# Linear attention and routed experts in one kernel: the inter-chunk products of a quad move into the next quad, and the state's sums with them

## Chip, cores and metric

One core of one Trainium2 chip runs the whole program. The metric is the device time of one execution in microseconds (us); lower is better. The kernel before was measured three times in a comparison: 363.81 us median, 362.58 to 365.19.

## What is computed

The input x is 8 sequences of 1024 tokens with 128 features, float32. It is normalized over the features (xn), and two branches are added to it:

```
x = L0_attn_x;  xn = _layernorm(x, axis=-1)
x = x + _L0_attn_ref(xn, W_qkv, W_o) + _L0_ffn_ref(xn, centroids, ln_g, ln_b, w1, b1, w2, b2)
# attention: 16 heads of 8 features, chunks of 64 tokens, keys normalized over their head
inter = einsum('bhde,bthe->bthd', S, q_c)
scores = where(causal, einsum('bthd,bshd->bhts', q_c, k_c), 0.0)
intra = einsum('bhts,bshd->bthd', scores, v_c)
S = S + einsum('bthd,bthe->bhde', v_c, k_c)          # the state, carried from chunk to chunk
# experts: each token goes to the one of 8 experts with the largest affinity
h = relu(layernorm(x)*g+b @ w1.T + b1);  out = sigmoid(affinity) * (h @ w2.T + b2) + x
```

## The kernel before

The tokens are 64 tiles of 128 tokens (two chunks of 64 each). Four tiles (four sequences, one pair of chunks) make a quad, and there are 16 quads, n = 0 to 15; even quads hold sequences 0 to 3, odd ones 4 to 7. Each quad is worked on in two halves, h = 2n and 2n+1, of two tiles each. All engines run one program each, written out by hand in the order in which it is issued, and they meet at semaphores; no scheduler moves anything. So what stands behind a waiting instruction on its engine waits too.

In the loop over h the engines do this for quad n:

- TensorE (PE): `scores(h)` for the half (64 small products into four PSUM banks `sc`); projections of the next quad: `kT_project(n+1)`, `q_project(n+1)`, `v_project(n+1)`, and `k_transpose(n+1)`; `state_step(n)`, what the two chunks of the quad add to the state; `inter_first(n)` and `inter_second(n)`, state times queries for the first and the second chunk; `products(h-1)`, masked scores times values of the half before; `output(n-1)`, the product with W_o; and transposes of rows (`x_transpose`) or, from quad 7, of the experts' weights (`w1_transpose`, `w2_transpose`). For odd n up to 7 come the expert affinities, and for n = 3, 5, 7, 9 three small products that rank the tokens.
- VectorE (DVE): `score_mask(h)` reads the score banks, multiplies by the causal mask and writes `pr`. PE can't begin `scores(h+1)` before it, because the banks are the same. For h below 18 ScalarE and GpSimd take one of the four banks (`score_copy`, `mask_scores`), and from quad 9 DVE takes all four. DVE also masks the state steps (`dstate_first`, `dstate_second`), makes the keys' variance `k_var(n+1)` from `sq`, its reciprocal root (`k_rstd`), the scaled values `vp` (`v_scale`), adds the output to x (`result(n-1)`), and does the layernorm's statistics, routing (`choose`, `count`, `ranks`, `places`, and from quad 9 the steps from `tiles_of_experts` to `slots_placed`) and, from quad 8, `b1_fold`.
- ScalarE (ACT): copies from PSUM to SBUF: `kT_copy`, `y_copy(n-1)`, `kn_copy(n+1)`, then `k_square` (writes `sq`), `k_root`, four `q_expand`, `q_copy`, half of the values' spreading (`values_across`), the transposed rows.
- GpSimd (POOL): up to quad 8 the state's two sums (`state_middle`, `state_end`), a bank of the mask, five tiles of layernorm and the values' other half; from quad 3 the scatter of rows to their expert's slots by indirect DMA (`send_rows`), paced by semaphores of other engines. From quad 9 the state's sums are DVE's.
- SyncE (SP): loads of tokens and expert weights, stores of results, each behind a semaphore.

PSUM has eight banks: four for scores, FA (queries, second state step, transposes), FB (keys, values, transposes) and two Y banks (first state step, then the attention of a quad, then its output). A bank is written anew only when the engine that reads it is done: `q_project` waits for `dstate_second`, `v_project` for `kn_copy`, the transposes into FA for `q_copy` and those into FB for `v_scale`.

After the last quad come 71 tiles of rows sorted by expert: load, transpose, up, relu, down, scatter-add. Their loop is not touched; only its entry (`se_scale`, `se_weights` of the first tiles) moves.

Of the kernel before, what the change touches and what calls it, by code (L numbers as in the profile page):

```python
# [19 lines left out]
def moe_attention_kernel(nc, x, w_qkv, w_o, centroids, ln_g, ln_b, w1, b1, w2, b2, out):  # L20
    B, L, D = x.shape
    E, F, _ = w1.shape
    P = 128
# [47 lines left out]
    with ctx:  # L71
# [25 lines left out]
        b2b = tokens[:, 0:E * D].rearrange("p (e d) -> p e d", d=D)  # L97
        lbb = tokens[:, CW:CW + E * D].rearrange("p (e d) -> p e d", d=D)
# [52 lines left out]
        dstate = sb("dstate", [P, NC, HALF, GW])  # L151
# [57 lines left out]
        banks = [ctx.enter_context(nc.psum_tensor(f"bank{i}", [P, BANK], F32)) for i in range(4)]  # L209
        FA, FB, Y = banks[0], banks[1], banks[2:4]  # L210
# [22 lines left out]
        def out_early(n):  # L233
            return n % 2 == 1 and n < 9
# [12 lines left out]
        def _(sp):  # L247
# [49 lines left out]
            for n in range(NQ - 1):  # L297
# [5 lines left out]
                if n == 6:  # L303
                    stored(n - 1)
                    sp.dma_start(lbb, ln_b.partition_broadcast(P)).then_inc(s("lb_in"), 16)
# [5 lines left out]
                if n and out_early(n):  # L311
                    store_quad(n - 1)
# [3 lines left out]
                if n and not out_early(n):  # L316
                    store_quad(n - 1)
# [28 lines left out]
        def _(pool):  # L346
# [79 lines left out]
            def state_middle(n):  # L426

                half = n % 2
                pool.wait_ge(s("dsta_sb"), n + 1)
                reach(pool, s("inter_ps"), n)  # L430
                if n < 2:
                    pool.tensor_copy(smid[:, :, :], dstate[:, 0, :, :]).then_inc(s("smid_ready"), 1)
                else:
                    pool.tensor_tensor(smid[:, :, :], state[:, half * HALF:(half + 1) * HALF, :], dstate[:, 0, :, :],
                                       ALU.add).then_inc(s("smid_ready"), 1)

            def state_end(n):
                half = n % 2
                pool.wait_ge(s("dstb_sb"), n + 1)
# [3 lines left out]
                pool.tensor_tensor(state[:, half * HALF:(half + 1) * HALF, :], smid[:, :, :], dstate[:, 1, :, :],  # L443
# [3 lines left out]
            for h in range(ROUTED):  # L447
                n = h // 2
                mask_scores(h)
                if h % 2 == 0:  # L450
                    state_middle(n)
                    state_end(n)
# [9 lines left out]
                else:  # L462
# [4 lines left out]
                    if n >= 3:  # L467
                        send_rows(2)
            for h in range(ROUTED, NH):
                n = h // 2  # L470

                pool.wait_ge(s("sc_ps"), h + 1)
                send_rows(1)
                if h % 2 == 0:
                    pool.wait_ge(s("av_ps"), h)
                    send_rows(1)
                    if n + 1 < NQ:
                        pool.wait_ge(s("q_ps"), n + 2)
                        send_rows(1)
                elif n + 1 < NQ:  # L480
                    pool.wait_ge(s("v_ps"), n + 2)
                    send_rows(1)
                    pool.wait_ge(s("out_ps"), n)
# [20 lines left out]
        def _(act):  # L504
# [129 lines left out]
            for h in range(NH):  # L634
# [3 lines left out]
                if h % 2 and more:  # L638

                    q_expand(n + 1, 0)  # L640
                    q_expand(n + 1, 1)
                if h and by_act(h):
                    score_copy(h)
                if h % 2 == 0:
                    if more:
                        kT_copy(n + 1)
                    if norm:
                        ln_root(n + 2)
# [5 lines left out]
                    if norm:  # L654
                        ln_norm(n + 2, (5, 6))
                    if n in (2, 4, 6, 8):
                        second_root(n // 2 - 1)
                else:
                    if more:
                        k_root(n + 1)  # L660
                        for j in range(2, J):
                            q_expand(n + 1, j)
                    if n < 8 and n % 2 == 1:
                        affT_copy(n // 2)
                    if more:
                        q_copy(n + 1)
# [65 lines left out]
        def _(dve):  # L732
# [129 lines left out]
            def dstate_first(n):  # L862
                dve.wait_ge(s("ds_ps"), n + 1)

                reach(dve, s("smid_ready"), n)
                nc.vector.tensor_tensor(dstate[:, 0, :, :], Y[n % 2][:, 0:HALF * GW].rearrange("p (i k) -> p i k", k=GW),
                                        bcast(smask[:, :], 1, HALF), ALU.mult).then_inc(s("dsta_sb"), 1)
# [611 lines left out]
```

## Time and profile before

| what | value |
|---|---|
| median of 3 runs | 363.81 us (362.58 to 365.19) |
| profiled execution | 363.22 us |
| its span | 361.4 us |
| what lies around the span | 1.8 us |
| granted TensorE clock | 0.992 of full over the span |
| quads 1 to 15 with the entry of the experts | 25.09 to 216.88 us of the span |
| experts' tiles | 216.88 us to the end |

The span is one execution by the hardware profiler; every duration below is of it. A quad is counted from the start of its `scores(2n)` on PE to that of the next.

### The profile page before, as it was taken

What the parts mean: (1) busy time and instruction counts of PE and PEld (TensorE: products, weight loads), DVE (VectorE), ACT (ScalarE), POOL (GpSimd) and SP (SyncE); (2) the same over time, 40 slices, a digit from 0 to 9 for tenths busy, and PEclk for the clock granted to TensorE, in tenths of its full rate; (3) what the DMA queues carried; (4) which work ended last, traced back from release to release, by engine and by line L of the source; (5) the groups of instructions that cost most, each with busy time, mean ns of one, the idle gap of its engine ahead of it and who ended that gap; (6) DMA issues with size and microseconds to landing.
All of it is one profiled execution on the core that took longest, in us unless ns stands there. A gap on an engine that the chain in (4) does not pass through costs nothing. (4 is left out here: it accounts for less than half of the span.)

```text
span 361.4 us, 17478 instructions
## 1 busy us (share of the span) xinstructions
PE 341.2 (94%) x6868; PEld 293.5 (81%) x6868; DVE 283.6 (78%) x799; ACT 241.7 (67%) x657; POOL 250.2 (69%) x245
## 2 busy tenths in 40 slices
PE   7799999989899999999999989999999999999990
PEld 7466776777587787777877878999999999999990
DVE  8887898898785988977878786788887778877760
ACT  4788677777667657666665735766677667766660
POOL 3388567889886865455455503888887888888884
PEclk9999999999999999999999999999999999999996
DMA  7403213021433233255233225555555555555420
GB/s 203 103 22 92 63 38 86 26 77 54 128 98 92 91 93 91 82 149 152 93 99 100 78 58 137 69 72 72 68 64 77 72 76 67 70 75 61 37 23 0
DMA packets 46705, 28.99 MB, mean 80 GB/s; under 512 B 5096, under 2 KB 44320, under 8 KB 46624
## 3 DMA queue, kind: packets, MB, share of 16 engines
q1 hardware_dynamic: 34352, 19.34, 19.6%
q0 software_dynamic: 12272, 8.54, 17.1%
q8 instruction: 55, 0.90, 1.1%
q14 instruction: 26, 0.21, 0.2%
HBM read 14.53 MB, written 13.78 MB: 78 GB/s over the span
## 5 line engine op out<-in xcount | busy, mean ns | idle before, releaser
L495 POOL DMA_INDIRECT out_dram<-qx,rows x71 | 112.7, 1588 | 36.0 <-issue 21.9
L695 ACT ACTIVATE qx<-sc,b1T 128x128 f32<-128x128 f32 x280 | 79.8, 368 | 40.4 <-PE sc L1424 40.4
L421 POOL DMA_INDIRECT slots_d<-rows,pos_i x64 | 62.8, 981 | 41.3 <-PE bank L1331 10.7
L857 DVE TENSOR_TENSOR pr<-sc,causal 128x1536 f32<-128x1536 f32 (+2 forms) x33 | 63.5, 1926 | 16.3 <-PE sc L1277 16.2
L1432 PE MATMUL bank<-tokens,qx 128*128 128x128 f32 x568 | 75.2, 276 | 0.7 <-ACT qx L695 0.7
L1424 PE MATMUL sc<-wide,tokens 128*128 128x128 f32 x560 | 74.1, 275 | 0.4 <-issue 0.4
L1432 PEld LDWEIGHTS bank<-tokens,qx 128*128 128x128 f32 x568 | 69.0, 192 | 1.1 <-ACT qx L695 1.1
L1424 PEld LDWEIGHTS sc<-wide,tokens 128*128 128x128 f32 x560 | 68.2, 192 | 0.6 <-issue 0.6
L1016 DVE COPY tokens<-xT 128x1024 f32 x71 | 53.3, 752 | 0.2 <-issue 0.2
L1277 PEld LDWEIGHTS sc<-qx,kT 32*64 32x64 f32 x2048 | 32.9, 130 | 16.8 <-issue 16.4
L1031 DVE SCALAR_TENSOR_TENSOR qx<-bank,rows,qx 128x128 f32<-128x128 f32 x71 | 24.8, 350 | 27.2 <-PE bank L1432 26.5
L1277 PE MATMUL sc<-qx,kT 32*64 32x128 f32 x2048 | 41.3, 279 | 2.3 <-issue 1.2
L538 ACT ACTIVATE qx<-bank,gmask 128x512 f32<-128x512 f32 x64 | 40.0, 679 | 0.9 <-PE bank L1203 0.8
L1331 PE MATMUL bank<-pr,vz 128*32 128x64 f32 x2048 | 37.4, 221 | 1.0 <-issue 0.8
L1331 PEld LDWEIGHTS bank<-pr,vz 128*32 128x32 f32 x2048 | 31.1, 110 | 6.0 <-issue 4.8
L413 POOL TENSOR_TENSOR pr<-pr,causal 128x512 f32<-128x512 f32 x18 | 22.9, 1273 | 7.6 <-ACT pr L569 7.2
L391 POOL TENSOR_SCALAR rows<-tokens,mv,rstd 128x128 f32<-128x128 f32 x35 | 27.5, 795 | 0.1
L1023 DVE SCALAR_TENSOR_TENSOR qx<-tokens,rows 128x128 f32<-128x128 f32 x71 | 24.5, 345 | 2.0 <-ACT rows L706 1.8
L603 ACT ACTIVATE y<-bank 128x512 f32<-128x512 f32 x16 | 9.6, 597 | 21.4 <-PE bank L1331 21.4
L1010 DVE TENSOR_SCALAR wide<-rows 128x128 f32<-128x128 f32 x71 | 19.6, 278 | 3.2 <-issue 2.7
L683 ACT ACTIVATE wide<-sc 128x128 f32<-128x128 f32 x69 | 20.2, 293 | 0.0
L1225 PEld LDWEIGHTS bank<-wqkv,xT 128*128 128x128 f32 x128 | 15.5, 191 | 4.4 <-issue 3.4
(167 smaller groups left out, 531.4 us busy)
## 6 DMA issues: line engine op xcount, KB each, us to landing
rows<-slots_d SPq DMA_DIRECT2D x71, 66.0 KB, 2.0
out_dram<-tokens SPq DMA_DIRECT2D x16, 256.0 KB, 2.7
tokens<-in_L_attn_x_dram SPq DMA_DIRECT2D x7, 512.0 KB, 4.2
w1raw<-in_L_ffn_w_dram SPq DMA_DIRECT2D x8, 256.0 KB, 3.3
w2raw<-in_L_ffn_w_dram SPq DMA_DIRECT2D x8, 256.0 KB, 2.9
out_dram<-qx,rows POOLq DMA_INDIRECT x71, 3.4
slots_d<-rows,pos_i POOLq DMA_INDIRECT x64
slots_d<-empty SPq DMA_DIRECT2D x9, 66.0 KB
```

The lines of the kernel that those rows point to most:

```text
L391: last = pool.tensor_scalar(rows[:, t, 0:D], xin[:, c, b, :], mv[:, t, 0:1], rstd[:, t:t + 1], ALU.subtract, ALU.mult)
L421: pool.indirect_dma_start(slots_d, bass.IndirectOffsetOnAxis(ap=pos_i[:, t:t + 1], axis=0), rows[:, t, :], None)\
L495: pool.indirect_dma_start(out_rows, bass.IndirectOffsetOnAxis(ap=xs[:, a, D + 2:D + 3].bitcast(U32), axis=0), ye[:, a, :], None, bounds_ch ...
L538: ins = nc.scalar.activation(qx[:, n % 2, :, j, :], FA[:, :].rearrange("p (i t) -> p i t", t=P), ACT.Copy, scale=gmask[:, j * DK:j * DK + 1])
L695: last = nc.scalar.activation(ht[:, k % 2, c * P:(c + 1) * P], inner(k)[:, c * P:(c + 1) * P], ACT.Relu, bias=b1T[:, bass.ds(e * FC + c, 1)])
L857: nc.vector.tensor_tensor(pr[:, h % 2, a:G, w].rearrange("p g (j t) -> p g j t", t=CH), sc[:, a * BANK:G * BANK].rearrange("p (g w) -> p g ...
L1016: nc.vector.tensor_copy(ws[:, k % 3, :], wts[:, bass.ds(e * WE, WE)]).then_inc(s("ws_ready"), 1)
L1031: nc.vector.scalar_tensor_tensor(out=ye[:, a, :], in0=banks[k % 2][:, 0:D], scalar=xs[:, a, D + 1:D + 2], in1=yb[:, k % 2, :], op0=ALU.mul ...
L1277: last = mm(SC[g][CH * up:CH * (up + 1), at:at + PAIRS * CH], kT[r, n % 2, tok], qx[r, n % 2, i, 2 * up:2 * up + 2, CH * c:CH * (c + 1)], ...
L1331: last = mm(Y[half][SW * g:SW * (g + 1), i * P + CH * c:i * P + CH * (c + 1)], vz[:, half, c, i, g, p, :], pr[:, h % 2, g, k:k + CH], star ...
L1424: last = mm(inner(k)[:, c * P:(c + 1) * P], ws[:, k % 3, c * P:(c + 1) * P], xsT[:, k % 2, :], start=True, stop=True)
L1432: last = mm(banks[k % 2][:, 0:D], ht[:, k % 2, c * P:(c + 1) * P], ws[:, k % 3, F + c * D:F + (c + 1) * D], start=(c == 0), stop=(c == FC ...
```

## The change

The order is rewritten on all engines.

- PE: `inter_first(n-1)` and `inter_second(n-1)` now stand in quad n, behind `kT_project(n+1)` and ahead of `state_step(n)`. Behind `products(2n-1)` come `k_transpose(n+1)`, `q_project(n+1)` and `v_project(n+1)` in a row, and then `scores(2n+1)`. `output(n-1)` always stands in the second half, first behind the scores. The products now clear a Y bank's accumulation, where `inter_first` did.
- Banks: Y, FA and FB lie in one tensor, so that the two state steps of a quad are neighbours and one DVE instruction of 128x512 masks both (`dstates`) in the place of two of 128x256. `dstate` has two buffers. In the last two quads, which need one step alone, it is still 128x256.
- State's sums: `state_end(n-1)` stands in quad n ahead of `state_middle(n)`, on POOL and on DVE.
- DVE: in the first half `score_mask(2n)`, the layernorm's inverse, `dstates(n)`, the sums, then `k_var(n+1)`, routing or slots, `b1_fold`, `k_rstd(n+1)`, `v_scale(n+1)`; in the second half `score_mask(2n+1)`, `result(n-1)` and the rest. In quads 1, 3, 5, 7 statistics and `result` stand ahead of `score_mask(2n+1)`.
- `b1_fold` waits for the weights' load and not for their transpose, and writes its product to `affT`.
- ACT: one `q_expand`, `k_root` and two more `q_expand` come in the first half, behind `k_square`; `score_copy(2n+1)`, the last `q_expand` and `q_copy` follow. `ln_root` comes first in a quad.
- POOL and SP: the scatters wait on other semaphores and end with quad 14; stores all stand behind `v_ps`; the first of the experts' broadcast loads comes two quads earlier.

The core of the diff:

```diff
-        dstate = sb("dstate", [P, NC, HALF, GW])
+        dstate = sb("dstate", [P, 2, NC, HALF, GW])
-        FA, FB, Y = banks[0], banks[1], banks[2:4]
+        Y, FA, FB = (banks[0], banks[2]), banks[1], banks[3]
...
 # POOL
                 if h % 2 == 0:
+                    if n:
+                        state_end(n - 1)
                     state_middle(n)
-                    state_end(n)
...
 # ACT, first half
                         kn_copy(n + 1)
                         k_square(n + 1)
+                        q_expand(n + 1, 0)
+                        k_root(n + 1)
+                        q_expand(n + 1, 1)
+                        q_expand(n + 1, 2)
...
 # DVE
+                    if more:
+                        k_var(n + 1)
...
-                    if n >= 8 and n + 1 < NQ:
+                    if n >= 8 and more:
                         b1_fold(n - 8)
-                else:
-                    if more:
-                        k_var(n + 1)
-                    score_mask(h)
                     if more:
                         k_rstd(n + 1)
                         v_scale(n + 1, FB)
+                    if n == NQ - 2:
+                        b1_fold(E - 1)
+                else:
...
+                    score_mask(h)
...
 # PE
                 if h % 2 == 0:
                     if more:
                         kT_project(n + 1)
+                    if n:
+                        inter_first(n - 1)
+                        inter_second(n - 1)
                     state_step(n)
                     if h:
                         products(h - 1)
-                    inter_first(n)
                     if more:
                         k_transpose(n + 1)
-                    if n and out_early(n):
-                        output(n - 1)
-                    if more:
                         q_project(n + 1)
+                        v_project(n + 1, FB)
                 else:
+                    if n:
+                        output(n - 1)
                     products(h - 1)
-                    if more:
-                        v_project(n + 1, FB)
-                    inter_second(n)
-                    if n and not out_early(n):
-                        output(n - 1)
```

TensorE in quad 10, from its first scores to the next quad's, before (`sc<-qx,kT` scores, `xT,wqkv` keys and then queries, `vp,kn` state step, `pr,vz` products, `qT,state` and `qT,smid` the inter-chunk sets, `ident,kT` the keys' transposes, `wqkv,xT` values, `wo,y` output):

```order
L1277 MATMUL sc<-qx,kT 64x128 x32
L1212 MATMUL bank<-xT,wqkv 128x512
L1258 MATMUL bank<-vp,kn 64x64 x16
L1331 MATMUL bank<-pr,vz 32x64 x32
L1298 MATMUL bank<-qT,state 64x64 x8
L1218 MATMUL bank<-ident,kT 128x128 x4
L1203 MATMUL bank<-xT,wqkv 128x512
L1277 MATMUL sc<-qx,kT 64x128 x32
L1331 MATMUL bank<-pr,vz 32x64 x32
L1225 MATMUL bank<-wqkv,xT 128x128 x4
L1309 MATMUL bank<-qT,smid 64x64 x8
L1340 MATMUL bank<-wo,y 128x128 x4
```

In both kernels the transposes of w1 and w2 follow, and then the next scores. The same stretch of the changed kernel:

```order
L1286 MATMUL sc<-qx,kT 64x128 x32
L1221 MATMUL bank<-xT,wqkv 128x512
L1306 MATMUL bank<-qT,state 64x64 x8
L1317 MATMUL bank<-qT,smid 64x64 x8
L1267 MATMUL bank<-vp,kn 64x64 x16
L1339 MATMUL bank<-pr,vz 32x64 x32
L1227 MATMUL bank<-ident,kT 128x128 x4
L1212 MATMUL bank<-xT,wqkv 128x512
L1234 MATMUL bank<-wqkv,xT 128x128 x4
L1286 MATMUL sc<-qx,kT 64x128 x32
L1348 MATMUL bank<-wo,y 128x128 x4
L1339 MATMUL bank<-pr,vz 32x64 x32
```

Both inter-chunk sets and the values' projection moved ahead of the second scores, and behind these stand four groups instead of six (w1 and w2 among them in both).

VectorE in quad 10, from the first mask to the last, before (`pr<-sc` the masks, `kvar<-sq` is `k_var`, `wide` the slots' step, `w1raw` or `affT` and `b1T` are `b1_fold`):

```order
L857 TENSOR_TENSOR pr<-sc,causal 128x2048
L866 TENSOR_TENSOR dstate<-bank,smask 128x256
L871 TENSOR_TENSOR dstate<-bank,smask 128x256
L879 TENSOR_TENSOR smid<-state,dstate 128x256
L884 TENSOR_TENSOR state<-smid,dstate 128x256
L989 TENSOR_SCALAR cnt<-cnt 128x8
L990 TENSOR_TENSOR wide<-cnt,iotk 128x568
L898 SCALAR_TENSOR_TENSOR w1raw,fold<-w1raw,tokens 128x128 x4
L902 TENSOR_TENSOR b1T<-smallT,fold 128x4
L829 TENSOR_REDUCE kvar<-sq 128x64
L857 TENSOR_TENSOR pr<-sc,causal 128x2048
```

And in the changed kernel:

```order
L864 TENSOR_TENSOR pr<-sc,causal 128x2048
L876 TENSOR_TENSOR dstate<-bank,smask 128x512
L885 TENSOR_TENSOR state<-smid,dstate 128x256
L892 TENSOR_TENSOR smid<-state,dstate 128x256
L836 TENSOR_REDUCE kvar<-sq 128x64
L998 TENSOR_SCALAR cnt<-cnt 128x8
L999 TENSOR_TENSOR wide<-cnt,iotk 128x568
L907 SCALAR_TENSOR_TENSOR affT,fold<-w1raw,tokens 128x128 x4
L911 TENSOR_TENSOR b1T<-smallT,fold 128x4
L841 RECIPROCAL krs<-kstd 128x64
L851 TENSOR_TENSOR vp<-bank,krs 128x512
L864 TENSOR_TENSOR pr<-sc,causal 128x2048
```

`kvar` moved ahead of the slots' step and of `b1_fold`, and `krs` and `vp`, which stood behind the second mask, now stand ahead of it.

## Rows read from the trace of the kernel before

**Rows 1.** Windows: length, busy us of PE, PEld, DVE, ACT, POOL; clock, DMA share, GB/s

```profile
104.02:117.20 13.18, 13.18 (x368) 9.96 (x368) 8.60 (x21) 9.14 (x18) 9.14 (x10) 1.00 0.39 108
25.09:129.57 104.48, 100.92 (x2858) 76.49 (x2858) 86.15 (x250) 76.97 (x156) 81.47 (x98) 1.00 0.26 74
129.57:205.35 75.78, 74.42 (x2101) 57.90 (x2100) 62.44 (x140) 49.36 (x97) 40.32 (x43) 1.00 0.35 105
205.35:216.88 11.53, 10.12 (x388) 8.89 (x388) 8.84 (x20) 4.77 (x9) 2.35 (x3) 1.00 0.31 80
```

**Rows 2.** Timeline of TensorE in quad 4 (start, duration, engine, line)

```profile
64.18 1.21 PE L1277 MATMUL sc<-qx,kT 32*64 32x128 f32 x64
65.31 1.13 PE L1212 MATMUL bank<-xT,wqkv 128*128 128x512 f32 x2
66.37 0.69 PE L1258 MATMUL bank<-vp,kn 64*64 64x64 f32 x32
66.99 1.10 PE L1331 MATMUL bank<-pr,vz 128*32 128x64 f32 x64
68.02 0.68 PE L1298 MATMUL bank<-qT,state 64*64 64x64 f32 x16
68.64 0.66 PE L1218 MATMUL bank<-ident,kT 128*128 128x128 f32 x4
69.13 1.02 PE L1203 MATMUL bank<-xT,wqkv 128*128 128x512 f32 x2
70.08 1.21 PE L1277 MATMUL sc<-qx,kT 32*64 32x128 f32 x64
...
72.25 1.16 PE L1225 MATMUL bank<-wqkv,xT 128*128 128x128 f32 x8
73.34 0.68 PE L1309 MATMUL bank<-qT,smid 64*64 64x64 f32 x16
...
75.11 1.09 PE L1169 MATMUL bank<-ident,rows 128*128 128x128 f32 x8
```

**Rows 3.** Timeline of VectorE in quad 10

```profile
144.25 2.29 DVE L857 TENSOR_TENSOR pr<-sc,causal 128x2048 f32<-128x2048 f32 x1 [1.41 <-PE sc L1277]
...
148.25 0.16 DVE L989 TENSOR_SCALAR cnt<-cnt 128x8 f32<-128x8 f32 x1
...
149.23 0.29 DVE L898 SCALAR_TENSOR_TENSOR w1raw<-w1raw,tokens 128x128 f32<-128x128 f32 x1
...
150.36 0.68 DVE L829 TENSOR_REDUCE kvar<-sq 128x64 f32<-128x512 f32 x1
150.95 2.28 DVE L857 TENSOR_TENSOR pr<-sc,causal 128x2048 f32<-128x2048 f32 x1
153.15 0.54 DVE L834 RECIPROCAL krs<-kstd 128x64 f32<-128x64 f32 x1
153.78 0.69 DVE L844 TENSOR_TENSOR vp<-bank,krs 128x512 f32<-128x512 f32 x1
```

**Rows 4.** Timeline of ScalarE in quad 10

```profile
148.38 0.60 ACT L598 ACTIVATE kn<-bank 128x512 f32<-128x512 f32 x1 [0.57 <-PE bank L1218]
149.01 0.63 ACT L551 ACTIVATE sq<-kn 128x512 f32<-128x512 f32 x1
```

**Rows 5.** Timeline of VectorE in quads 2 and 3

```profile
43.39 0.30 DVE L953 TENSOR_TENSOR tmp_nt<-rstd 128x16 f32<-128x16 f32 x1
...
46.09 1.75 DVE L857 TENSOR_TENSOR pr<-sc,causal 128x1536 f32<-128x1536 f32 x1
...
50.21 0.16 DVE L936 COPY scan<-ohb 128x8 bf16<-128x8 bf16 x1
...
52.93 1.73 DVE L857 TENSOR_TENSOR pr<-sc,causal 128x1536 f32<-128x1536 f32 x1
```

**Rows 6.** Timeline of TensorE, its inter-chunk set in quad 5 and products in quad 12

```profile
81.47 0.68 PE L1298 MATMUL bank<-qT,state 64*64 64x64 f32 x16 [1.14 <-DVE dstate L866]
...
171.76 0.76 PE L1331 MATMUL bank<-pr,vz 128*32 128x64 f32 x38 [0.45 <-issue]
```

More of the change, by code:

```diff
@@ L208, in moe_attention_kernel @@
         SC = [sc[:, g * BANK:(g + 1) * BANK] for g in range(G)]
-        banks = [ctx.enter_context(nc.psum_tensor(f"bank{i}", [P, BANK], F32)) for i in range(4)]
-        FA, FB, Y = banks[0], banks[1], banks[2:4]
+        bank = ctx.enter_context(nc.psum_tensor("bank", [P, 4 * BANK], F32))
+        banks = [bank[:, i * BANK:(i + 1) * BANK] for i in range(4)]
+        Y, FA, FB = (banks[0], banks[2]), banks[1], banks[3]
         RANK = HALF * GW
@@ L230, in inner, with with_affinities, with_ranks, step_of @@
             return SC[2 + k % 2] if k else FA
-        def out_early(n):
-            return n % 2 == 1 and n < 9
+        def with_affinities(n):
+            return n % 2 == 1 and n < 8
+        def with_ranks(n):
+            return n in (3, 5, 7, 9)
+        def step_of(n, c):
+            return dstate[:, n % 2, c ^ n % 2, :, :]
         block = ctx.enter_context(nc.Block())
@@ L637, in _ @@
                 norm = n + 1 < NCH
[L638 to L643, printed above, removed]
                 if h % 2 == 0:
+                    if norm:
+                        ln_root(n + 2)
+                    if h and by_act(h):
+                        score_copy(h)
                     if more:
@@ L658, in _ @@
                 else:
+                    if by_act(h):
+                        score_copy(h)
                     if more:
[L660 to L663, printed above, removed]
+                        q_expand(n + 1, 3)
+                        q_copy(n + 1)
+                    if with_affinities(n):
                         affT_copy(n // 2)
-                    if more:
-                        q_copy(n + 1)
                     if more:
@@ L1098, in _ @@
                         v_scale(n + 1, FB)
+                    if n == NQ - 2:
+                        b1_fold(E - 1)
+                else:
+                    if with_affinities(n):
+                        if stat:
+                            ln_stats(n + 3, range(4, B))
+                            ln_moments(n + 3)
+                        result(n - 1)
+                    score_mask(h)
+                    if n == NQ - 1:
+                        se_scale(0)
+                        se_scale(1)
+                    if n and not with_affinities(n):
+                        result(n - 1)
                     if n == NQ - 1:
@@ L1106, in _ @@
                         se_weights(1, e[3])
-                        se_scale(0)
-                        se_scale(1)
-                    if n and not out_early(n):
-                        result(n - 1)
                     if n == NQ - 2:
@@ L1118, in _ @@
                         second_rstd(n // 2 - 1)
[L1119 removed]
+                    if stat and not with_affinities(n):
                         ln_stats(n + 3, range(4, B))
                         ln_moments(n + 3)
[L1122 removed]
+                    if with_affinities(n):
                         aff_copy(n // 2)
```

125 lines of the change are left out of this document (57 added, 68 removed).

## The prediction

> **What bounds the kernel now.** I read the windows first, quad by quad, then TensorE's timeline, then VectorE's and ScalarE's around the waits of TensorE. The windows show PE busy for 100.92 of 104.48 us in quads 1 to 8 and for 74.42 of 75.78 in quads 9 to 14 [rows 1]: so PE's row of work fills the time, and the order of its instructions is what counts. The busy time alone proves little, for a matmul's end is modelled and covers short waits. So the timeline of PE in quad 4, where nothing waits for long, is to be read from start to start [rows 2]: scores 1.13, keys 1.06, state step 0.62, products 1.03, an inter-chunk set 0.61, keys' transposes 0.49, queries 0.95, values 1.09, the row transposes 1.03 with a short wait (the quad after starts at 76.14). The whole quad takes 11.96.
>
> What PE waits for, where it waits, is VectorE: 1.14 us for the masked state step in quad 5 [rows 6]. DVE is second: 86.15 of 104.48 us, and 62.44 of 75.78 [rows 1]. Per quad of 9 to 14 that is 10.4 of 12.6 us. So DVE has some 2 us to spare in a late quad, and less in the early ones. In the late quads it spends them waiting for scores (1.41 us ahead of a mask, [rows 3]). Nobody waits there, because two masks a quad, each 2.2 us, stand about half a quad apart. The experts' loop is not touched.
>
> **The change, part by part.** PE alone. The number of products stays. Set ahead, the two inter-chunk sets and the state step share one tile shape, and PE changes its shape less often. The price of a change of shape is in the difference of like groups (values 1.09 where a set of 64x64 follows, queries 0.95 where scores follow), about 0.1. I take 0.55 for a set that a set follows (ends: 0.50 and the 0.61 of the row), 1.0 for the values and 1.09 for the output, of the same form as the values. From the start of a quad: keys 1.13, first set 2.19, second 2.74, state step 3.29, products 3.91, keys' transposes 4.94, queries 5.43, values 6.38, second scores 7.4; then output 8.5, products 9.6, transposes 10.6, next scores at 11.7. So PE's own work would shrink from 11.96 to 11.7 us.
>
> The Trainium skill, "TensorEngine Tiling (Array Packing)", section "Key Properties", says that a change of tiling mode, other than of tile, drains TensorE. The trace agrees with that as far as the 0.1 us goes; by the rule alone the change would be a gain of some 0.2 us a quad. It does not say what the new order does to the other engines.
>
> The halves are no longer equal. Before, the second scores came about halfway (70.08 of 64.18 to 76.14, [rows 2]). Now the first half has 7.4 us and the second 4.3. DVE's mask of the second half must be done before the next quad's scores, since they write the same banks; it has 4.3 less the scores' 1.2, which is 3.1 us, for 2.28 us of mask, if DVE is free when the scores end.
>
> It is not free. In the first half it now runs `k_var`, which waits for `sq`, ahead of everything else that is left. Quad 10, from its start: the first mask starts at 1.35, when the scores end, and takes 2.21 to the next start [rows 3], to 3.6. The state step ends on PE at 3.29 + 0.69 = 4.0; `dstates` at 128x512 I price as `vp`, the same shape from PSUM, 0.69 [rows 3], to 4.75. The two sums, about 0.4 each, to 5.6. Now DVE waits: the keys' transposes end at 4.94 + 0.66 = 5.6, `kn` takes 0.60 and `sq` 0.63 with the small step between [rows 4], so `sq` ends at 6.9. This wait, 1.3 us, is new: before, the slots' step and `b1_fold` lay over it. Then `k_var` 0.59 from start to start, to 7.5; the slots' step 0.98 (148.25 to 149.23), to 8.5; `b1_fold` 1.13 (149.23 to 150.36), to 9.6; `krs` 0.63 and `vp` 0.63, to 10.9; the second mask 2.28, to 13.2; and PE starts at 13.3 where it was ready at 11.7 [rows 3]. What is queued behind that wait is the chain to the mask, and PE waits for it 1.6 us in each quad.
>
> Quads 9 to 14 by this walk: 13.3 in quads 10 and 11, 13.1 in 12, 13.4 in 13 (what stands in the slots' place there is 0.8 to 1.1); 13.4 in 14, where a second `b1_fold` (1.13) stands in it; 14.0 in 9, with ten small routing steps at about 0.17. The sum is 80.5 against 75.78: **4.7 us more**.
>
> Early quads. In 2, 4 and 6 the same chain has `choose` in it, 2.1 us (43.39 to 46.09 less the 0.59 of `k_var`), and a mask of 1.75 [rows 5]: 7.5 + 2.1 + 1.26 + 1.75 = 12.6, next scores at 12.8. In 3 and 5 DVE comes late from that: after the mask still `result` (0.6) and 2.72 us of counting, statistics and moments (50.21 to 52.93, [rows 5]). Its mask starts at 3.2 and ends at 4.95, `dstates` at 6.1, queries go at 6.2 instead of 5.6. `kn` comes behind two rows of layernorm and `y` on ACT, at 6.9, so values go at 7.6 and `sq` ends at 8.2. Then `k_var` 0.6, two small steps 0.5, `krs` and `vp` 1.26, statistics and moments 1.4, `result` 0.6, mask 1.75: 14.4, next scores at 14.5, in quad 5 14.7. Quad 7 has no layernorm left and PE sets its end, as in its window of 13.18 where PE is busy throughout [rows 1]: 13.1. Quad 1: 7.5 + 1.26 + 1.4 + 0.6 + 1.75 and the wait for the root, 13.3. Quad 8: `b1_fold` and a short mask, with the queries' copy on ACT at 11.3 and the transposes behind it, 12.3. The sum is 13.3 + 12.8 + 14.5 + 12.8 + 14.7 + 12.8 + 13.1 + 12.3 = 106.3 against 104.48: **1.8 us more**. The ends: with DVE a little faster everywhere, 102; with every wait of ACT behind DVE added once more, 110.
>
> The entry of the experts: in quad 15 `b1_fold` no longer stands ahead of the mask, about 0.9 us sooner for the second scores, but two inter-chunk sets now stand after them, about 0.6: 11.2 for 11.53 [rows 1], **0.3 less**.
>
> Pauses: PE stops now and then in the middle of a group for nothing that the profile names, 0.45 in quad 12 [rows 6]; such pauses add up to some 4 us in quads 1 to 14. My walks have none. Behind the second scores they lie beside DVE's lateness and cost nothing, in front of the keys' transposes they come on top. I add **0.8** (ends 0 and 2.5).
>
> Free of cost: one `dstates` for two masks saves 0.1 us of DVE (2 x 0.41 against 0.69) and lies in front of the wait for `sq`. The Trainium skill, "Perfetto Trace Analysis", section "Optimizing Scalar/DVE Operations", gives DVE some 125 ns of overhead an instruction on PSUM, which would be the same 0.1 us a quad; it would count only where DVE is the bound, and here the wait swallows it. The state's sums a quad later stay on POOL before quad 9, which has room; if they were late, the inter-chunk sets would wait. SP's stores behind `v_ps` and POOL's scatters on other semaphores lie beside PE; if the last rows landed later, the first expert tile would wait.
>
> The sum: 363.2 (the profiled execution, beside a median of 363.8) + 4.7 + 1.8 - 0.3 + 0.8 = 370.2 us.
>
> **The rivals.** *PE stays the bound (faster).* If `sq` comes early enough or DVE's steps shrink, the quads go at PE's own pace: seven even quads and 9, 11, 13 at 11.7, three with affinities at 13.0, quad 1 at 12.5: 168.5 against 180.3; less 11.8, with the pauses some 3 back: 354. For it speaks PE's full row; against it that the chain after `sq` adds up to 6.3 us at its shortest in quad 10, and 6.9 + 6.3 is over 11.7. It decides if that sum falls below 4.8.
>
> *The halves trade evenly (no change).* Late quads lose the 1.6 us, but early quads gain what PE waited for, and pauses vanish into DVE's lateness: quads 9 to 14 at 13.1 (78.6, 2.8 more), 1 to 8 at 12.7 (101.6, 2.9 less): 363. For it speaks that quad 5 alone waits 1.14 now [rows 6], and that most of the pauses now fall beside a wait.
>
> *ScalarE or GpSimd takes over (slower still).* `q_copy` comes behind seven instructions that wait on `sq` and `k_var`; POOL is busy 81.47 of 104.48 us [rows 1], and in quads 3 to 6 its scatters push its part of the mask back. If that adds 0.7 us in each of quads 1 to 8, the time is 376. It decides from the point where POOL's mask comes later than the products behind the next state step.
>
> **How the numbers follow.** A measurement of this kernel can tell about 1% from no change, 3.6 us. The forecast of 370 has a chance of 0.52 in itself, the still slower case 0.14, the even trade 0.19, and PE's pace, whole or in half, 0.15. Of the forecast's own range (366 to 374) almost all is slower by over 1%. The range that should hold 8 in 10 reaches down into the even trade and up to the third rival: 360.5 to 376. Faster by over 1% 0.15, within 1% 0.20, slower by over 1% 0.65.
>
> **What would show it.** Right, if in quads 10 to 14 PE waits 1 to 2 us ahead of each first scores, released by DVE's mask; if DVE's `kvar` waits about 1.3 us for `sq`; if these quads take 13.1 to 13.5 us, with PE idle where it was full; and if quads 3 and 5 have a wait of the queries for `dstate`. Wrong, if the late quads take below 12.3, or the second mask starts as soon as its scores end.

## The result, and the profile after

The changed kernel takes 375.95 us (median of 4 runs, 375.0 to 377.15) where the kernel before takes 363.33 on the same chip: a ratio of 1.0337, 95% interval 1.0302 to 1.0372, slower. The forecast was 370.2 with a range up to 376.0, so the direction holds and the size was 5.8 us short; the measured time lies 0.05 us inside the range. The profiled execution has a span of 373.3 us against 361.4. (Of the kernels below, kvar_late was profiled in its one slow execution, with a lower clock of TensorE for some microseconds; its time is that of the others, and its quads 0, 13 and 15 are not read.)

The windows of the changed kernel, cut where the first scores of quads 1, 9, 15 and 0 start, to be held against [rows 1] (the columns are the same):

```profile
core 0: us, PE busy (x) PEld busy (x) DVE busy (x) ACT busy (x) POOL busy (x), PEclk, DMA share, GB/s
25.59:134.01 108.42, 100.32 (x2842) 75.31 (x2841) 83.39 (x241) 76.88 (x156) 79.54 (x96) 1.00 0.25 71
134.01:215.94 81.93, 72.02 (x2101) 56.09 (x2101) 64.14 (x146) 50.81 (x100) 43.84 (x46) 1.00 0.33 99
215.94:229.01 13.07, 11.23 (x418) 9.69 (x419) 8.33 (x12) 3.10 (x6) 0.15 (x1) 1.00 0.35 90
12.95:25.59 12.64, 9.05 (x251) 6.50 (x250) 11.51 (x37) 10.81 (x23) 8.44 (x12) 1.00 0.15 44
```

Quads 1 to 8 take 108.42 us (104.48 before, +3.9), quads 9 to 14 81.93 (75.78, +6.15), quad 15 13.07 (11.53, +1.55), quad 0 12.64 (12.13, +0.5). The experts' loop takes what it took. PE, busy for 74.42 of 75.78 us before, now idles 9.9 of 81.93. Its timeline in quad 10 shows where:

```profile
148.71 1.20 PE L1286 MATMUL sc<-qx,kT 32*64 32x128 f32 x64 [1.63 <-DVE pr L864]
149.84 1.12 PE L1221 MATMUL bank<-xT,wqkv 128*128 128x512 f32 x2
150.89 0.68 PE L1306 MATMUL bank<-qT,state 64*64 64x64 f32 x16
...
152.47 0.62 PE L1267 MATMUL bank<-vp,kn 64*64 64x64 f32 x25 [0.32 <-issue]
153.02 1.10 PE L1339 MATMUL bank<-pr,vz 128*32 128x64 f32 x64
154.05 0.66 PE L1227 MATMUL bank<-ident,kT 128*128 128x128 f32 x4
154.54 1.02 PE L1212 MATMUL bank<-xT,wqkv 128*128 128x512 f32 x2
155.41 1.16 PE L1234 MATMUL bank<-wqkv,xT 128*128 128x128 f32 x8
156.49 1.43 PE L1286 MATMUL sc<-qx,kT 32*64 32x128 f32 x64
...
160.47 0.60 PE L1245 MATMUL bank<-ident,w2raw 128*128 128x128 f32 x4
162.38 0.87 PE L1286 MATMUL sc<-qx,kT 32*64 32x128 f32 x37 [1.31 <-DVE pr L864]
```

The first half runs from 148.71 to 156.49 and no matmul in it waits for another engine (the 0.32 is a pause in the middle of a group, see below); the second is done at 161.1 and then PE waits 1.31 us for the second mask, where [rows 2] had no long wait. DVE's timeline of the same quad, to be held against [rows 3]:

```profile
149.95 2.29 DVE L864 TENSOR_TENSOR pr<-sc,causal 128x2048 f32<-128x2048 f32 x1 [0.79 <-PE sc L1286]
153.13 0.69 DVE L876 TENSOR_TENSOR dstate<-bank,smask 128x512 f32<-128x512 f32 x1 [0.89 <-PE bank L1267]
153.73 0.41 DVE L885 TENSOR_TENSOR state<-smid,dstate 128x256 f32<-128x256 f32 x1
154.28 0.42 DVE L892 TENSOR_TENSOR smid<-state,dstate 128x256 f32<-128x256 f32 x1
156.05 0.69 DVE L836 TENSOR_REDUCE kvar<-sq 128x64 f32<-128x512 f32 x1 [1.34 <-ACT sq L559]
...
156.84 0.78 DVE L999 TENSOR_TENSOR wide<-cnt,iotk 128x568 f32<-128x568 f32 x1
...
158.71 0.54 DVE L841 RECIPROCAL krs<-kstd 128x64 f32<-128x64 f32 x1
159.34 0.69 DVE L851 TENSOR_TENSOR vp<-bank,krs 128x512 f32<-128x512 f32 x1
159.95 2.28 DVE L864 TENSOR_TENSOR pr<-sc,causal 128x2048 f32<-128x2048 f32 x1
```

From `kvar` on DVE has no gap, and its mask ends at 162.2, when PE may go. In [rows 3] the second mask ends at 153.23, 2 us ahead of the next scores (155.18); here it ends 0.15 us ahead of them. The waits over the attention part (engine, line, released by: us in total, times, longest):

```profile
DVE kvar L836 <- ACT sq L559: 20.8, 14, 3.3
...
PE sc L1286 <- DVE pr L864: 11.1, 9, 1.6
PEld bank L1234 <- ACT kn L606: 9.3, 14, 0.7
```

The first row is the wait that the change adds (before it was 1.5 us in all), the second is its price on PE. The price is paid late: quads 9 to 14 have 8.7 us of the first and 7.2 of the second, quads 1 to 8 have 12.1 and 2.5. The third row costs nothing: it is the load of the values' weights, beside the queries' matmuls. The chain that ended last has changed owners too; its shares are by engine, and DVE had 2% and PE 5% of it before:

```profile
issue 30%; PE 28%; DVE 20%; POOL 12%; ACT 8%; POOLq 1%; DVEq 0%; ACTq 0%
```

### The profile page after: what moved, and what is told of

Its sections match the earlier page's. It is cut to its first block, busy times and chain, and to the rows that moved or that the text cites. A ratio compares the mean times of both kernels' runs of the same rounds, so it can differ in the third digit from the quotient of the medians.

```text
span 373.3 us, 17460 instructions
## 1 busy us (share of the span) xinstructions
PE 338.4 (91%) x6868; PEld 290.6 (78%) x6868; DVE 282.8 (76%) x786; ACT 241.8 (65%) x657; POOL 249.6 (67%) x244
## 4 chain that ended last, share of the span: by engine, by line
issue 30%; PE 28%; DVE 20%; POOL 12%; ACT 8%; POOLq 1%; DVEq 0%; ACTq 0%
POOL out_dram L503 12%; DVE pr L864 6%; PE bank L1339 6%; PE sc L1286 5%; PE bank L1221 4%; PE bank L1306 2%; PE bank L1267 2%; ACT sq L559 2%; DVE kvar L836 2%; PE bank L1348 2%; ACT kn L606 2%; PE bank L1317 2%; DVE stats L768 2%; PE bank L1227 2%; DVE krs L841 1%
## 5 line engine op out<-in xcount | busy, mean ns | idle before, releaser
L1025 DVE COPY tokens<-xT 128x1024 f32 x71 | 54.3, 766 | 0.1
L1286 PE MATMUL sc<-qx,kT 32*64 32x128 f32 x2048 | 40.4, 279 | 11.4 <-DVE pr L864 11.1
L546 ACT ACTIVATE qx<-bank,gmask 128x512 f32<-128x512 f32 x64 | 40.9, 677 | 0.3 <-PE bank L1212 0.3
L836 DVE TENSOR_REDUCE kvar<-sq 128x64 f32<-128x512 f32 x16 | 11.0, 686 | 21.2 <-ACT sq L559 21.2
```

Of the source, the lines that this page charges most:

```text
L546: ins = nc.scalar.activation(qx[:, n % 2, :, j, :], FA[:, :].rearrange("p (i t) -> p i t", t=P), ACT.Copy, scale=gmask[:, j * DK:j * DK + 1])
L1025: nc.vector.tensor_copy(ws[:, k % 3, :], wts[:, bass.ds(e * WE, WE)]).then_inc(s("ws_ready"), 1)
L1286: last = mm(SC[g][CH * up:CH * (up + 1), at:at + PAIRS * CH], kT[r, n % 2, tok], qx[r, n % 2, i, 2 * up:2 * up + 2, CH * c:CH * (c + 1)], ...
```

## The experiments

The ratios below are to the kernel before on the same chip. The changed kernel itself was measured in another comparison than its variants, which ran on three chips, and the medians of the kernel before lie between 363.3 and 364.9 us on these chips; so a difference in microseconds from the 375.95 is good to some 1.5 us.

### Taking k_var out of the way, and making DVE's row shorter

**kvar_late.** DVE's `k_var` behind everything that does not need it.

```diff
                     if stat:
                         ln_stats(n + 3, range(4))
-                    if more:
-                        k_var(n + 1)
...
                     if more:
+                        k_var(n + 1)
                         k_rstd(n + 1)
```

> The changed kernel, with VectorE's sum of the key squares (k_var, which waits for ScalarE's squares) moved behind choose, the slots' step and the fold of the biases, just ahead of k_rstd. Theory (VectorE's row from one mask to the next is the bound of a quad, and the idle 1.34 us ahead of k_var is part of it): the wait of k_var for sq goes, the masks end about 1.0 us earlier, so quads 9 to 14 take about 12.5 to 12.9 us each instead of 13.1 to 14.7, the even quads below 8 gain about 0.8 each, and the whole is 366 to 369 us. Rival 1 (TensorE's own order and its pauses set the quads, the wait at the scores is only where they show): within 1 us of 376. Rival 2 (ScalarE and GpSimd, through the late squares and what follows them, are the bound): within 1.5 us of 376, with a new wait of VectorE ahead of the values' scaling or of the mask.

Measured: 369.8 us, ratio to before 1.0125 (1.0056 to 1.0195), so 6 us of the 12.6 (nearly 8 by the ratios) are gone by the place of one instruction; the 366 to 369 are just missed. Quads 10 to 12 take 12.22, 12.33 and 12.19 us for 13.67, 13.51 and 12.97. Of `kvar` for `sq` no wait is left in quads 9 to 12, and the waits of PE for the mask there sum to 1.0 us. As accounts of the whole both rivals fall. But a part of the second is there. `kstd` on ScalarE waits for the later `kvar` (in quad 4 it starts 8.42 us after the quad's start for 7.64), and what stands behind it, the last `q_expand` and the queries' copy, comes later too. So `krs` waits 0.41 us for `kstd`, and PE's transposes wait for `qT` in quads 2, 4, 6, 8 and 9, from 27.91 to 147.95 us of the span:

```profile
PE bank L1178 <- ACT qT L554: 2.6, 3, 1.0
...
PE bank L1239 <- ACT qT L554: 1.9, 2, 1.3
```

That is why quads 4 and 6 gain 0.4 us instead of the 0.8 expected, quad 2 loses 0.3, and quad 9 still takes 13.94 us.

**fold1_after, fold1_before.** The same cut of DVE's work in either kernel: three of the four chunks of the biases' product are left out.

```diff
-                for c in range(FC):
+                for c in range(1):
```

> The changed kernel with one of the four chunks of the bias fold left in (three quarters of the b1 fold are not computed, the buffer is cleared once): about 0.65 us less of VectorE in each quad from 8 on. Theory (VectorE's row sets quads 8 to 14): its mask comes 0.65 us earlier and each such quad shortens by about that, 4 to 4.5 us in all, 371 to 373 us. Rival 1 (TensorE bounds): less than 1 us gained, 375 to 377. Rival 2 (ScalarE's squares set k_var, and all that lies ahead of it is free): the fold stands behind k_var in these quads, so this rival too gives a gain; it is told apart by the run with k_var later.

> The kernel before with the same three quarters of the bias fold left out. Theory (TensorE's row was the bound there and VectorE had slack in the second half, where the fold stood): 362.5 to 364, no change within 1 us. Rival (VectorE was the bound already in the kernel before, and the change only made it longer): a gain of 0.5 us a quad as in the changed kernel, 359 to 361 us.

Measured: 372.4 us for the changed kernel (ratio to before 1.0204, 1.0133 to 1.0276), 3.5 us less than with the whole fold (4.8 by the ratios), and 363.5 for the kernel before (0.9996, 0.9965 to 1.0027), nothing. Quads 10, 11 and 12 shorten by 0.64, 0.75 and 0.67 us for the 0.65 us (three chunks at 0.215 each) taken out, quad 9 by 0.65 and quad 8 by 0.41: in these late quads every microsecond of DVE is a microsecond of the quad. The kernel before had that slack, the changed one has not.

### The same chain, shortened on the other engines

**ktr_first.** DVE's order is left alone. The keys' transposes go ahead of the old products on TensorE, and ScalarE makes keys and squares before `y`, which needs those products.

```diff
+                    if more:
+                        kn_copy(n + 1)
+                        k_square(n + 1)
                     if n:
                         y_copy(n - 1)
                     if more:
-                        kn_copy(n + 1)
-                        k_square(n + 1)
...
+                    if more:
+                        k_transpose(n + 1)
                     if h:
                         products(h - 1)
                     if more:
-                        k_transpose(n + 1)
                         q_project(n + 1)
```

> The changed kernel with VectorE's order untouched; on TensorE the keys' transposes stand ahead of the old products instead of behind them, and on ScalarE the keys' copy and squares stand ahead of the copy of y. Theory (the chain from the squares over k_var, slots, fold, krs, vp and the second mask is the bound in quads 9 to 14): the squares end some 1.2 us earlier after a quad's start, k_var waits 0.1 to 0.4 us instead of 1.34, and the quads 9 to 14 lose about 0.9 to 1.1 us each as with k_var moved, although no instruction of VectorE changes its place: 368 to 371 us. Rival 1 (it was k_var's place in VectorE's row that cost, by something else than the wait for the squares): 374 to 377. Rival 2 (the products, now half a microsecond later, hold back y, the output and the next state step): the second halves grow by what the first lose, 373 or more.

Measured: 364.35 us (median of 12), ratio 1.0012 (0.9985 to 1.0039): no difference from the kernel before, 11.6 us less than the changed kernel, and better than was expected. The windows:

```profile
26.85:130.39 103.54, 100.95 (x2842) 76.55 (x2841) 84.53 (x242) 76.43 (x156) 79.85 (x95) 1.00 0.26 74
130.39:206.19 75.80, 72.76 (x2101) 57.25 (x2101) 63.52 (x141) 49.40 (x98) 42.77 (x45) 1.00 0.36 107
206.19:219.03 12.84, 11.37 (x418) 9.78 (x419) 8.33 (x12) 4.11 (x8) 0.96 (x1) 1.00 0.37 97
12.95:26.85 13.90, 10.56 (x251) 7.89 (x250) 11.84 (x41) 10.94 (x23) 8.55 (x12) 0.88 0.14 40
```

Quads 9 to 14 lose 6.1 us, as the theory had it, and quads 1 to 8 lose 4.9, which it had not counted (4, 6 and 8 take 12.05, 11.75 and 11.98 for 13.17, 13.18 and 13.14). DVE's timeline of quad 12, which starts at 169.63:

```profile
174.82 0.42 DVE L893 TENSOR_TENSOR smid<-state,dstate 128x256 f32<-128x256 f32 x1
175.50 0.69 DVE L837 TENSOR_REDUCE kvar<-sq 128x64 f32<-128x512 f32 x1 [0.25 <-ACT sq L559]
176.10 0.74 DVE L1008 TENSOR_TENSOR wide<-wide,cnt 128x568 f32<-128x568 f32 x1
...
178.56 0.69 DVE L852 TENSOR_TENSOR vp<-bank,krs 128x512 f32<-128x512 f32 x1
179.17 2.28 DVE L865 TENSOR_TENSOR pr<-sc,causal 128x2048 f32<-128x2048 f32 x1
```

The same two of the changed kernel, whose quad 12 starts at 175.89:

```profile
182.76 0.69 DVE L836 TENSOR_REDUCE kvar<-sq 128x64 f32<-128x512 f32 x1 [1.42 <-ACT sq L559]
...
186.44 2.28 DVE L864 TENSOR_TENSOR pr<-sc,causal 128x2048 f32<-128x2048 f32 x1
```

`kvar` stands at 5.87 us of its quad for 6.87, the mask at 9.54 for 10.55, and the quad takes 11.96 for 12.97. The next scores find it ready, as in most of these quads (in 9 to 14 PE waits 2.0 us in all for the mask, 7.2 in the changed kernel):

```profile
181.05 0.60 PE L1246 MATMUL bank<-ident,w2raw 128*128 128x128 f32 x4
181.59 1.27 PE L1287 MATMUL sc<-qx,kT 32*64 32x128 f32 x64
```

This is the change with all its early sets, as fast as the kernel before. So neither the sets ahead nor the values in the first half cost the time by themselves: the late squares did. In quads 10 to 12 kvar_late had repaired as much; what this kernel has over it stands in quads 1 to 8 (103.54 us for 106.10), where `kvar` and `kstd` now come early and no transpose of PE waits for `qT`.

### The values back in the second half

**v_second.**

```diff
                         q_project(n + 1)
-                        v_project(n + 1, FB)
                 else:
-                    if n:
+                    if n and with_affinities(n):
                         output(n - 1)
                     products(h - 1)
+                    if more:
+                        v_project(n + 1, FB)
+                    if n and not with_affinities(n):
+                        output(n - 1)
```

(On DVE `k_var` follows the fold; the second mask goes ahead of `krs`, `vp` and `result`.)

> The changed kernel, with the projection of the values taken out of the first half and put back into the second one, behind the products of the head before, and VectorE's order to go with it: k_var at the end of the first half, then the mask, k_rstd, v_scale, fold and result. The sets, the old products and the keys' transposes ahead of the queries stay. Theory (the first half grew because all of keys' scaling, values' scaling and the mask must follow one another inside it): the first half shortens by the 0.86 us of the values' matmuls on TensorE and by about 1.4 us on VectorE, and the second half has room for both, so quads 9 to 14 take about 12.4 to 12.7 us and the whole is 361 to 366 us, at the level of the kernel before. Rival 1 (the halves only trade: what leaves the first comes back in the second): 373 to 377. Rival 2 (the sets placed early, not the values, cost the time): the first halves stay at 7.2 us or more, 371 to 376.

Measured: 374.5 us, ratio 1.0246 (1.0174 to 1.0317): only 1.5 less than the changed kernel (3.3 by the ratios), so the 361 to 366 were wrong, and the number alone is that of the rivals. Quads 9 to 14 did what the theory says, 76.9 us in all, with 12.4 to 12.8 in 10 to 14. The loss is in the odd quads below 8, at 14.1 to 15.8 us, and one wait of quads 1 to 8 names it:

```profile
PE bank L1190 <- DVE tokens L899: 5.5, 4, 1.4
```

My order put DVE's `result` behind mask, `krs` and `vp`, and TensorE's affinities need it. A wait that the edit made, and no evidence on the change.

**mix, mix_shift32.** v_second, with the values in the first half in quads 1, 3, 5 and 7 (there DVE's order is that of kvar_late); the second with 32 tiny transposes more at TensorE's start.

```diff
+                    if with_affinities(n):
+                        v_project(n + 1, FB)
                 else:
...
-                    if more:
+                    if more and not with_affinities(n):
                         v_project(n + 1, FB)
```

> The changed kernel with k_var behind the fold everywhere; the values' projection, their scaling and krs stay in the first half only in the quads with affinities (1, 3, 5, 7), and are back in the second half in all others. Theory (VectorE's row in the first half, from the mask over the squares to the values and the second mask, is what the change made too long; in quads 1, 3, 5, 7 TensorE's second half is the full one, so the values belong in the first there): quads 9 to 14 as in v_second (73 to 77 us with pauses), the odd quads below 8 as in kvar_late (13.3 to 14.7), together 363 to 368 us. Rival (the early sets cost time of their own in the quads below 8, by the longer first half, whatever stands behind them): quads 1 to 8 stay at 107 or more, 368 to 371 us.

> The same with 32 tiny transposes at TensorE's start (its instruction stream 64 instructions further on). Theory (waits for instruction blocks): the same work between the pauses, the pauses at other places, the time up to 3 us to either side of mix. Rival: within 0.5 us of mix.

Measured: 368.9 us, ratio 1.0148 (1.0106 to 1.0191), and 370.8, ratio 1.0203 (1.014 to 1.0266). The first is 1 us above what its theory allowed and inside the rival's 368 to 371, though its parts fit the theory: quads 9 to 14 take 76.8 us, the odd ones below 8 13.3 to 14.9, and quads 1 to 8 together 106.1, below the rival's 107. The shift moved the pauses to other places, and the median by 1.8 us; the runs of the two overlap (368.0 to 370.4 and 369.7 to 373.5), so the 1.8 is not clear of their spread.

**mix_rf.** mix, with `result` ahead of the statistics.

```diff
+                        result(n - 1)
                         if stat:
                             ln_stats(n + 3, range(4, B))
                             ln_moments(n + 3)
-                        result(n - 1)
                     score_mask(h)
```

> mix, with VectorE's result of the quad before put ahead of the statistics and moments in quads 1, 3, 5 and 7. Theory (in quads 3 and 5 TensorE's affinities wait 0.75 to 0.9 us for the result, which stands behind 1.4 us of statistics): this wait goes, and quads 3 and 5 shorten by 0.5 to 0.8 us each, 1 to 1.5 us in all. Rival (the later moments push ScalarE's root and its rows back, and the row transposes wait for them instead): 0 to 1 us longer than mix.

Measured: 368.6 us, ratio 1.0122 (1.0065 to 1.0178), not to be told from mix. The wait of the affinities (1.9 us in three quads) is gone, and in its place PE waits 1.9 us at the scores for the mask, also three times, which neither theory nor rival had. Still, quads 1 to 8 take 104.99 us for 106.13 in the profiles, most of it in quad 5 (14.17 for 14.88); quads 9 to 14 take 77.74 for 76.79, with 3.8 us of pauses for 3.0. So the early gain may be real and hidden by pauses; the times of the whole show none.

### The pauses of TensorE

**shift32_after, shift64_after, shift32_before, shift64_before.** PE's work is the same; only its instruction stream is longer in front.

```diff
             keep_busy(22)
+            for _ in range(32):
+                nc.tensor.transpose(SC[3][0:32, 0:32], ident[0:32, 0:32], ident[0:32, 0:32])
```

> The changed kernel with 32 tiny transposes (32x32, nobody reads them) more at TensorE's start, where it is idle: nothing of the work changes, but all that TensorE issues later stands 64 instructions further on in its instruction stream. Theory (TensorE's pauses in the middle of a group, which end 1.2 to 1.5 us after a 16 KB block of instructions has landed, are waits for that block; they took about 3 us of quads 9 to 14 and of the tail together): the pauses come at other places of the work, a quarter of a block earlier (64 of 256 instructions), and the time moves by -3 to +2 us, 373 to 378. Rival (the pauses belong to those places of the work, for example to a transfer or to a neighbour engine's use of a port): they stay at 125.6, 151.9, 193.3, 218.7 and 225.3 us and the time stays within 0.5 us of 376.

> The changed kernel with 64 such transposes, so the stream is shifted by half a block (128 instructions). Theory: other places again, none where they were, and another time, between 372 and 378 us. Rival: as for the shift by 64 instructions, the same places and the same time.

> The kernel before with 32 such transposes at TensorE's start. Theory: the pauses of the kernel before (97.4 us with 1.5 us, 171.0 with 0.7, and smaller ones) move to other places, some of them into its tail, which had none; 362 to 368 us. Rival: they stay, and the time stays within 0.5 us of the kernel before.

> The kernel before with 64 such transposes, half a block. Theory: as for 32, at yet other places, 361 to 369 us; the four shifted kernels together give the share of the 12 us between before and after that is luck of the stream's position: expected 1 to 3 us. Rival: nothing moves.

Measured: the changed kernel takes 374.4 and 378.0 us (ratios 1.0305, 1.0253 to 1.0357, and 1.0411, 1.0354 to 1.0469), the kernel before 363.35 and 368.2 (0.9991, 0.9961 to 1.0021, and 1.0117, 1.0086 to 1.0148). Nothing of the work changed, and the time moves by -1.5 to +4.8 us. Not all of that is pauses. With 64 transposes the front itself is longer (the first scores of the kernel before start at 13.99 for 12.96 us), and in the profiled execution quad 0 has a granted clock of 0.87 for 1.00 and takes 13.39 us for 12.13; in the changed kernel with 64 it has 0.88 and takes 13.71 for 12.64. The pauses alone (stops of over 0.25 us inside a group of like instructions, each counted from one weight load's start to the next) sum to 4.6, 2.8 and 6.2 us in the kernel before with 0, 32 and 64 transposes, and to 5.1, 2.9 and 5.7 in the changed one. Every pause is at another place. The mean over the three positions is 376.1 us for the changed kernel and 364.95 for the one before: 11.2 us apart, so 1 to 2 us of the 12.6 are luck of the position (pauses and the clock of quad 0 together). The tail of the changed kernel, weight loads of PE (in brackets the idle time ahead):

```profile
218.60 0.25 PEld L1339 LDWEIGHTS bank<-pr,vz 128*32 128x32 f32 x11
219.39 0.82 PEld L1339 LDWEIGHTS bank<-pr,vz 128*32 128x32 f32 x53 [0.54 <-issue]
...
226.64 0.49 PEld L1339 LDWEIGHTS bank<-pr,vz 128*32 128x32 f32 x32 [1.27 <-issue]
```

and the same tail with 32 transposes in front, where both are gone and one of 0.62 us stands in the scores:

```profile
218.80 0.70 PEld L1288 LDWEIGHTS sc<-qx,kT 32*64 32x64 f32 x43
220.12 0.41 PEld L1288 LDWEIGHTS sc<-qx,kT 32*64 32x64 f32 x21 [0.62 <-issue]
...
223.91 0.94 PEld L1341 LDWEIGHTS bank<-pr,vz 128*32 128x32 f32 x64
```

Quad 15 takes 11.62 us there for 13.07. In the stretch of the changed kernel from 224.3 to 225.5, ahead of the second of its pauses, the page of DMA queues shows one packet of 0.02 MB:

```profile
q8 instruction: 1, 0.02, 5.0%
```

In these six kernels there are 40 such pauses; 39 of them end 1.2 to 1.6 us after such a packet has landed and the last 1.7. The packets land 3.2 us apart at the least and about 5 us as a rule, so this is not chance. The rival (pauses bound to a place in the work) falls.

## Why the prediction was right, and where it was short

*The number.* 375.95 lies at the very edge of the range of 360.5 to 376, and that it lies inside is luck: the same kernel with its stream shifted takes 374.4 and 378.0 us. The forecast itself was 5.8 us short; the terms below say where.

*The mechanism.* The prediction named the wait of `k_var` for `sq`, with the chain to the mask queued behind it, and PE waiting at the next first scores. All three are in the trace: 1.34 us (forecast 1.3), the mask at 11.24 (10.9), the wait of PE 1.63 and 1.31 (1.6). Three kernels that shorten that chain by different means (its order on DVE, its work, its start on PE and ScalarE) gain 6.1, 3.5 and 11.6 us, and the kernel before gains nothing from the second. One sign came under another name: in quads 3 and 5 the queries wait 0.39 and 0.61 us, but for `rank`, the step of DVE behind `dstate` for which they wait as well.

*PE alone.* Set after set starts 0.52 us apart (0.55 taken), and the whole of 11.7 us is met where nothing else binds: quad 6 of ktr_first, with the same products as quad 4 of before [rows 2], takes 11.75 us for 11.96 (its values take 0.98 from start to start for 1.09, with scores behind them and no set). Its quad 12 takes 11.96 where quads 10 and 14 of before took 12.30 and 12.28. The Trainium skill's drain at a change of tiling mode ("TensorEngine Tiling (Array Packing)", section "Key Properties") would by itself have made the change a gain of 0.2 us a quad. The trace of ktr_first agrees, with these 0.2 to 0.3 us; in the changed kernel the waits cover them.

*Quads 9 to 14, +4.7 with 0.8 for pauses; measured +6.15.* Quads 10 to 12 and 14, at 13.67, 13.51, 12.97 and 13.14, lie within 0.4 of the walk (13.3, 13.3, 13.1, 13.4). The rest is quad 9 (14.70 for 14.0) and quad 13 (13.94 for 13.4), with pauses of 0.59 and 0.71 in the first halves of 10 and 13. In quad 9 `kvar` starts 7.36 us after the quad's start for the 6.9 of the walk, and the eight routing steps behind it take 2.02 us. The 0.8 for pauses was meant for quads 1 to 14; with the 1.12 of quad 8 those ahead of DVE's lateness come to 2.4, near the upper end of its 0 to 2.5.

*Quads 1 to 8, +1.8; measured +3.9.* This term was mis-sized. Quad 8 (13.14 for 12.3) holds a pause of 1.12 in its first half; quads 4 and 6 take 13.2 for 12.8, quads 3 and 5 15.0 and 15.2 for 14.5 and 14.7. The walk had missed that in quads 3 and 5 TensorE's affinities wait for `result`. It had `result` in DVE's row, ahead of the mask, but not as something that PE waits for; in quad 5 the second mask is done at 93.5 us, and PE, late from this wait, comes to the next scores at 94.37:

```profile
91.92 1.07 PE L1190 MATMUL bank<-xT,smallT 128*32 128x512 f32 x8 [0.75 <-DVE tokens L899]
```

mix_rf shows that with this wait taken away the mask is late instead, by 1.9 us for 1.9; whether anything is gained is left open there.

*The entry of the experts, -0.3; measured +1.55.* The work itself did as forecast (11.2 us; quad 15 takes 11.62 with the pauses shifted, one of 0.76 still in it). The step that failed is "pauses", which had been counted for quads 1 to 14 alone; the trace of before has none in its tail. The two pauses of the changed kernel there, 0.65 and 1.38 us from weight load to weight load, explain the rest.

*Quad 0, not in the forecast, +0.5.* PE's waits in its first half, for the keys' copy and for `dstate`, are 0.2 us longer each (0.94 for 0.75, 0.70 for 0.52), and ahead of its row transposes PE now waits 1.07 us for `qT`.

*The rivals.* PE as the bound is ruled out by the rows. The even trade failed since quad 5's 1.14 us [rows 6] came back as other waits of PE for DVE (affinities 0.75, ranks 0.61, the mask 0.83, all in quad 5). The third had the right number, 376, for the wrong reason: in quads 1 to 8 no wait of PE is put down to POOL, and only short ones to ScalarE (the values' weight load for the keys' copy, 5.4 us over 8 quads, beside running matmuls; `qT` 0.25 at most). kvar_late shows that its mechanism is near all the same: there the late `qT` holds PE up by 4.5 us.

*What is left open.* mix still takes 5 us more than before. Its profiled execution has 8.0 us of pauses for 4.6, and quad 0 takes 1.8 us more than before, where its clock is 0.88; the sum fits, but no run separated the two. Why the pauses grew there is not shown.

## What to carry to other kernels

When instructions are put in a row on the engine that bounds, walk the in-order engine that serves it from its first new wait to the last thing its neighbour needs: an early instruction with a late input (here a 0.7 us reduction) puts its wait in front of everything behind it, and moving it, or its producer, was worth 6 to 11 us here. A wait that is only passed on is worth little: in quad 5 of the change it came back in full at other consumers, and in mix_rf waits of the same sum stood at the mask instead. And two kernels that differ by 1% in time may differ only by where their instruction stream is cut and by the clock of their first microseconds; shift the stream by some dozens of idle instructions, and compare the granted clock stretch by stretch, before believing in such a difference.

## What the runs showed of the hardware

- TensorE waits for its own instructions. They come in blocks (q8: 55 packets, 0.90 MB, so 16 KB each), and PE stops now and then, for 0.3 to 1.8 us in the six kernels (2.2 in kvar_late), until 1.2 to 1.7 us after the next one has landed. The Trainium skill, "Runtime: NRT & Kernel Launch", section "Instruction fetch mechanics", has a crossing of such a block mostly hidden. The trace agrees for most blocks: 4 to 8 of the 55 or so are followed by a pause of over 0.25 us. It does not agree that the rest is small for this stream of small matmuls: these pauses sum to 2.8 to 6.2 us in the six kernels, with another sum at every shift.
- The granted clock fell to 0.88 over quad 0 in several variants (ktr_first above, also v_second, mix and the changed kernel with 64 transposes), and the quad took 13.7 to 13.9 us for 12.64 in the changed kernel, where the clock stayed at 1.00. From 20 to 24 us of kvar_late it was 0.50, which is the lower of the two levels (1.2 GHz), after PE had waited 1.68, 1.08 and 0.94 us in front of three groups. In the profile of the changed kernel the same three waits stand and the clock stayed at 2.4 GHz. It was also 0.50 from 192.7 to 195.9 us of kvar_late and from 160.4 to 163.6 of mix_shift32, soon after pauses of 2.2 us (ended at 191.4) and 1.9 (ended at 158.7): there a wait for instructions may have cost more than its own length. The four runs of the changed kernel have a mean clock of 0.985 to 0.994, so part of their 2 us of spread is likely this.
